# The last 512 rows of a macaron layer on eight cores: x1 + be2 made ahead, ACT's layer norm parts at once, the second MoE by two tiles and then one by one, and a shorter test of the experts

## What is computed

```python
def ffn(x):                       # the MoE; used before and after the attention layer
    out_shared = square(relu(x @ Ws1)) @ Ws2              # 1024 -> 512 -> 1024
    logits = x @ Wr                                       # 8 experts
    top_vals, top_idx = top_k(logits, 2)
    prob = trunc(einsum('tk,tke->te', softmax(top_vals), one_hot(top_idx, 8)))
    out_routed = sum over experts e of prob[:, e] * (square(relu(x @ W1[e])) @ W2[e])
    return out_shared + out_routed

x = x + 0.5 * ffn(layernorm(x))
h = layernorm(x)                                          # tokens of the attention layer
    a = attention(h)                                      # 16 heads of 64, distance bias, Wo, bo
    h1 = layernorm(h + a, g1, be1)
    h2 = layernorm(relu(h1 @ W1 + b1) @ W2 + b2 + h1, g2, be2)   # 1024 -> 4096 -> 1024
x = x + h2
x = x + 0.5 * ffn(layernorm(x))
```

## Time and profile before

| what | value |
|---|---|
| time, median of 3 runs | 1472.01 us (1470.12 to 1521.51) |
| the profiled execution: its own time | 1472.74 us |
| its span, slowest core (core 7) | 1471.2 us |
| spans of the eight cores | 1447.5 to 1471.2 us |
| PE busy | 1302.5 us (89%), 6452 matmuls |
| DVE busy | 790.7 us (54%) |
| ACT busy | 832.0 us (57%) |
| chain that ended last | PE 70%, DMA 8%, DVE 8%, ACT 6%, issue 6%, SP's queue 2% |

### The profile page before, as it was taken

The page is one execution under the profiler, slowest core; times in us unless marked ns, Lnnn a source line. Parts: engine busy times, 40 slices in busy tenths (PEclk is TensorE's granted clock), DMA queues, the critical chain, the costliest instruction groups (busy, mean ns, idle before and its releaser), DMA issues.

```text
span 1471.2 us, 20223 instructions; the slowest of 8 cores (1447.5 to 1471.2 us)
## 1 busy us (share of the span) xinstructions
PE 1302.5 (89%) x6452; PEld 609.8 (41%) x6452; DVE 790.7 (54%) x1272; ACT 832.0 (57%) x1157; POOL 38.3 (3%) x68
## 2 busy tenths in 40 slices
PE   3779679999989999998899999988999999779985
PEld 2334224444433544443335444334454444444432
DVE  5745214554467644358585443775834449670074
ACT  4555337777755765765557567555675666512211
POOL 1011100000000000000000000000000000000000
PEclk9989999999999999999999999999999999999997
DMA  9957989999923522214544222146432323674433
GB/s 238 196 125 140 133 121 131 133 116 115 129 75 105 170 75 101 81 73 154 168 132 128 76 96 90 55 161 211 126 115 74 106 76 78 212 224 171 145 130 116
DMA packets 115214, 187.64 MB, mean 128 GB/s; under 512 B 55822, under 2 KB 92692, under 8 KB 104088
## 3 DMA queue, kind: packets, MB, share of 16 engines
q1 hardware_dynamic: 86536, 154.74, 34.8%
q0 software_dynamic: 28560, 31.45, 17.8%
HBM read 178.86 MB, written 45.09 MB: 152 GB/s over the span
## 4 chain that ended last, share of the span: by engine, by line
PE 70%; DMA 8%; DVE 8%; ACT 6%; issue 6%; SPq 2%; DVEq 0%; ACTq 0%; POOL 0%; POOLq 0%
PE PS L243 70%; DMA Y<-widea 3%; ACT EB L806 2%; DMA HT<-SG 2%; DMA VV<-x 1%; DVE AT L846 1%; DVE EB L812 1%; DMA Y<-SG 1%; DVE Y L1000 1%; DVE sm L224 1%; DVE SG L912 1%; SPq L68 1%; SPq L66 1%; DVE sm L226 1%; ACT RT L842 1%
## 5 line engine op out<-in xcount | busy, mean ns | idle before, releaser
L806 ACT ACTIVATE EB<-PS 128x1024 bf16<-128x1024 f32 x512 | 520.4, 1022 | 323.1 <-PE PS L243 319.8
L812 DVE TENSOR_TENSOR EB<-EB,DP 128x1024 bf16<-128x1024 bf16 x512 | 352.5, 690 | 423.2 <-ACT EB L806 421.8
L243 PE MATMUL PS<-RG,H 128*128 128x512 bf16 x1280 | 314.3, 387 | 28.0 <-ACT H L1033 8.9
L243 PE MATMUL PS<-EB,VV 128*128 128x512 bf16 x1024 | 309.6, 384 | 22.1 <-DVE AT L846 19.1
L243 PE MATMUL PS<-HT,RG 128*128 128x256 bf16 (+1 forms) x1536 | 289.0, 334 | 29.7 <-DMA HT<-SG 13.1
L243 PE MATMUL PS<-QP,KT 128*128 128x512 bf16 x1024 | 309.5, 384 | 5.4 <-ACT EB L806 3.8
L243 PEld LDWEIGHTS PS<-HT,RG 128*128 128x128 bf16 x1536 | 153.3, 100 | 151.5 <-issue 39.0
L243 PEld LDWEIGHTS PS<-RG,H 128*128 128x128 bf16 x1280 | 125.8, 99 | 187.8 <-issue 46.0
L243 PEld LDWEIGHTS PS<-QP,KT 128*128 128x128 bf16 x1024 | 100.4, 99 | 132.0 <-issue 16.1
L243 PEld LDWEIGHTS PS<-EB,VV 128*128 128x128 bf16 x1024 | 96.9, 99 | 139.6 <-issue 47.1
L1033 ACT ACTIVATE H<-PS,sm 128x512 bf16<-128x512 f32 (+1 forms) x160 | 94.8, 599 | 72.6 <-PE PS L243 72.0
(11 more groups left out here) (124 smaller groups left out, 826.1 us busy)
## 6 DMA issues: line engine op xcount, KB each, us to landing
RG<-wcW SPq DMA_DIRECT2D x64, 1024.0 KB, 4.9
RG<-wcWo SPq DMA_DIRECT2D x8, 1024.0 KB, 11.3
wcW<-W1a POOLq DMA_DIRECT2D x8, 1024.0 KB, 22.7
wcW<-W2a POOLq DMA_DIRECT2D x8, 1024.0 KB, 19.8
Y<-x1sp SPq DMA_DIRECT2D x16, 512.0 KB, 4.1
XT<-x1sp SPq DMA_DIRECT2D x16, 512.0 KB, 4.6
RG<-wcS SPq DMA_DIRECT2D x8, 1024.0 KB, 6.7
out<-Y SPq DMA_DIRECT2D x16, 512.0 KB, 3.6
```

The source lines that it names most:

```text
L243: return s.on("tensor", lambda e: e.matmul(out, lhsT, rhs, start=first, stop=last, skip_group_check=True), wait=wait, inc=inc)
L806: te = s.on("scalar", lambda e: e.activation(eb, po, AF.Exp, bias=-12.0, scale=1.0), wait=[tm, self.e_free[k], self.tok_consts])
L812: self.tok_p[k] = s.on("vector", lambda e: e.tensor_tensor(eb3, eb3, dp, ALU.mult), wait=[te, self.tok_dp])
```

## The change

Only the last block (b = 3), where `lagging` is 0, is changed, but for two steps of the test that phase A's router shares.

- First LN: `SG` of tile tt is made in step tt, not in step tt+1.
- x1 of all four tiles is loaded at once after the first LN, into four pieces of `KT` (K is no longer read by then), and be2 is added to all four (4 additions of 1.22 us each, L946) directly after the first LN. `XT` is not used in this block; a tile's second LN goes from L956 straight to L968.
- `ln3_out` (ACT's part of the third LN, and the transposing DMA) is issued as soon as the tile's statistics are, not after those of the next tile.
- The second MoE takes tiles (0, 1), then 2, then 3.
- `router` takes the maximum of `rp1 + rw` (16 numbers a row) instead of the table of 128; the table is made after the flag. In the last block the two `Y` additions of the last tile stand inside the router, behind the exponential on ACT.

```diff
-    def router(self, s, wait, k):
+    def router(self, s, wait, k, mid=None):
...
         te = s.on("scalar", lambda e: e.activation(self.rd, self.rd, AF.Exp), wait=[t])
+        if mid is not None:
+            mid()
...
-        v(lambda e: e.tensor_tensor(PR3, LT3, bc(self.v2), ALU.is_ge))
-        v(lambda e: e.tensor_tensor(PR3, PR3, bc(self.rw), ALU.mult))
-        v(lambda e: e.tensor_tensor(eq3, eq3, bc(self.rp1), ALU.mult))
-        v(lambda e: e.tensor_add(self.PR, self.PR, self.eq1))
+        v(lambda e: e.tensor_add(self.rden, self.rp1, self.rw))
         fm = self.fm[:, k:k + 1]
-        return v(lambda e: e.tensor_reduce(fm, self.PR, AX.X, ALU.max))
+        t = v(lambda e: e.tensor_reduce(fm, self.rden, AX.X, ALU.max))
+
+        def table():
+            v(lambda e: e.tensor_tensor(PR3, LT3, bc(self.v2), ALU.is_ge))
...
+        return t, table
...
-            if tt:
+            j = tt if not self.lagging else tt - 1
+            if 0 <= j < 4:
...
-        tx = self.x1_again(s, b, 0, self.tok_xt_free)
+        if b < 3:
+            txs[0] = self.x1_again(s, b, 0, XT[0], self.tok_xt_free)
+        else:
+
+            XT = [self.KT[:, 2 * D * k:2 * D * k + 2 * D].bitcast(F32) for k in range(4)]
+            for tt in range(4):
+                t = self.x1_again(s, b, tt, XT[tt], [self.q_used[31]])
+                txs[tt] = s.on("vector", lambda e, x=XT[tt]: e.tensor_add(x, x, gc[:, D:2 * D]),
+                               wait=[t, self.tok_gc])
+                yield 1.22
...
             late = tt, Y[tt], c, mv, t
+            if not self.lagging:
+                self.ln3_out(s, b, HTt, *late)
+                late = None
...
-        for lo in (0, 2):
-            yield from self.need(("xn3", b, lo + 1), 3)
-            tr = [self.tok(("xn3", b, tt)) for tt in range(lo + 2)]
+        for lo, hi in ((0, 2), (2, 4)) if b < 3 else ((0, 2), (2, 3), (3, 4)):
+            yield from self.need(("xn3", b, hi - 1), 3)
+            tr = [self.tok(("xn3", b, tt)) for tt in range(hi)]
+            nn = 128 * (hi - lo)
...
+            if 4 * b + tt == 15:
+
+                tflag, table = self.router(
+                    s, [tlt], 1, lambda: [self.moe_out(s, b, tt, dh, *outs[dh]) for dh in range(2)])
+                bk = self.fill_bank()
+                self.tok_flag2 = self.router_flag(s, tflag, [self.bank_free[bk]], 1, self.bank(bk))
+                self.bank_free[bk] = self.tok_flag2
+                table()
```

More of the change, by code:

```diff
@@ L971, in ln3_out, with x1_again @@
         self.put(("xn3", b, tt), tr)
-    def x1_again(self, s, b, tt, wait):
+    def x1_again(self, s, b, tt, dst, wait):
         i = 4 * b + tt
-        return s.dma("sync", "xt", self.XT[:, :], self.x1_d[128 * i:128 * i + 128, :], wait=wait)
+        return s.dma("sync", "xt" if b < 3 else "xt%d" % tt, dst, self.x1_d[128 * i:128 * i + 128, :], wait=wait)
     def post_fill(self, s, b):
@@ L1089, in post_fill @@
                 yield 1
-            if lo:
+            if hi == 4:
                 self.ring_load(s, tm)
             bk = self.fill_bank()
-            for tt in (lo, lo + 1):
+            for tt in range(lo, hi):
                 for dc in range(NDC):
@@ L1106, in post_fill @@
                 self.ht_free = [tm, tx]
-                if b == 3:
-                    tflag = self.router(s, [tlt], 1)
-            for tt in (lo, lo + 1):
-                i = 4 * b + tt
+            for tt in range(lo, hi):
+                outs = []
                 for dh in range(2):
```

69 lines of the change are left out of this document (39 added, 30 removed).

## The result

The changed kernel takes 1454.56 us, median of 5 runs (1453.86 to 1457.86), the kernel before 1470.12 (1466.79 to 1521.51) on the same chip. The ratio is 0.9905, 95% interval 0.9883 to 0.9926: 14.0 us or 0.95% less, within 2% as forecast, but nearly three times the gain forecast and outside the range of 1462 to 1472.5.

The account below looks back on a forecast made before the run. PE's own work was 70% of the chain, so only waits around the first LN and from the second MoE on could move. +1.0 - 4.7 - 2.2 + 1.0 = -4.9 from 1472.0 gave 1467 us, range 1462 to 1472.5.

Parts of the forecast that it names:

- First place: First LN to FFN up pass: early start lost to a wait of some 5 us for W1's piece 1; +1.0 us.
- wcS1: Start of second MoE: its first weights, queued behind tile 1's transposing DMA, land at 1430.6 and set it; -1.0 us.
- The half clock: Second MoE: 16 first down matmuls take 5.0 us instead of 6.55, -1.6; allowance of 0.8 for the single tiles.
- Single tiles: Second MoE: PE does tile 2 while tile 3 is prepared; 0.056 us per matmul, up pass 1.8 us.
- Rival 1: Second MoE: single tiles do not pay, 128-column matmuls being bound by their weight load; +3.4, 1470.5 us; chance 0.2.
- Test: From the copy of the last logits to the flag: 6.2 us instead of 8.4; -2.2 us.
- The end: After the flag: the table makes DVE last at the barrier, with 0.6 us of cover; +1.0 us.
- Rival 2: W1's piece 1 and wcS1 land early, clock stays up, down pass 3.6 us; 1463 us; chance 0.17.
- Rival 3: First LN: W1 and x1 loads delay tile 3's transposing DMA, second half 7 us late; 1473 us; chance 0.1.
- Rival 4: Row work is hidden anyway: only the test and the 128-column passes gain; 1471 us; chance 0.05.

Follow-up runs that it names:

- e1: Changed kernel with the first LN's SG made one tile late again, as before; 1457.03 us.
- e6: Changed kernel with the second MoE's first weights wcS1 loaded ahead of tile 1's transposing DMA; 1461.90 us.
- e8: Changed kernel with ACT's part of the third LN issued one tile late again, as before; 1455.58 us.
- e7: Changed kernel with x1 loaded tile by tile again and be2 added in the second LN, as before; 1465.21 us.
- e9: e6 plus 15 matmuls into an unused bank ahead of the second MoE's first down pass, results unread; 1457.24 us.
- e3: Changed kernel with the four table steps ahead of the flag's copy again; 1458.45 us.
- e4: Changed kernel with the last tile's two Y additions behind the maximum again, so its output DMA is as late as before; 1457.17 us.
- e10: e4 without the output DMA of the last tile, whose 128 output rows are not written; 1463.24 us.

## Why the prediction was wrong

The sum was -4.9 and the last block gained 12.5 us. Taken at the same cuts, in medians of the cores, the missing 7.6 are (the rows are rounded):

| step | forecast | measured | missed |
|---|---|---|---|
| up to the start of the second MoE | +1.0 - 1.0 = 0 | -1.4 | 1.4 |
| from there to its first down pass | -0.8 | -1.8 | 1.0 |
| from there to the last up pass's end | -2.9 | -5.5 | 2.6 |
| from there to the flag | -2.2 | -2.5 | 0.3 |
| flag to end | +1.0 | -1.4 | 2.4 |

- **First place: right in mechanism.** The stop moved from the transposing DMA to piece 1 of W1 and the early start was lost; e1 shows it by undoing it. The size was +0.3 in the median instead of +1.0, and +2.9 on core 7, where PE waited 8.04 us for piece 1, against "some 5". The landing of one load scatters by 2.3 us between cores, and one row of it had been read.
- **wcS1: right in mechanism**, the chain of core 5 has it and e6 takes it away. The MoE started 0.7 us sooner than the term said, beside the 0.7 of the first place: it landed 4.8 to 5.4 us after its issue, where the prediction had taken 6.2.
- **The half clock: the main miss, and the step that failed.** The prediction gave the first down pass 5.0 us, halfway between the rows of 6.55 and 3.61, because "the gap ahead of them is now half as long", and the single tiles an allowance of 0.8. The gap did shrink, from 2.2 to 2.96 us on the cores of before to 1.1 to 1.7 in after. But the pass took the whole 3.61 on every core (3.40 where the trace has 15 of the 16 matmuls), and both single tiles ran at full clock: 1.4 + 0.8 of the 2.6. The up pass ahead of them, which the prediction left at its old length, took 5.3 us instead of 6.2 (medians), which is 0.9 of the 1.0 in the second row. So 3.1 of the missing 7.6 us are the clock's. It isn't a price to be interpolated.
- **What the clock went by.** The length of the stop ahead of a pass alone doesn't set it. Over all runs, 16 down matmuls took 3.61 after every stop up to 2.1 us, and 4.9 to 6.6 after every one of 3.5 or more. In between both are found: after 2.58 us 4.93 and 6.55 on cores 6 and 7 of before, 3.61 on cores of e8, and e7 has both after the same 2.0 us ahead of a pass of 8. What differs between before and e8 is the stop ahead of the up pass, 5.5 to 5.7 us against 2.9. In e7 that one was 6.1 to 7.2, only the second was short (0.9 to 1.8), and the pass took 3.61 too. So either stop made short was enough, on all cores but one (core 0 of e8: 4.58 for 15 of them, after 2.96); in after both are shorter. What decides between the two outcomes of one length stays open. That it is PE's standing still that costs, e9 shows by filling the stop.
- **Single tiles: right, and the row of 0.056 us held.** 32 matmuls took 1.95 with the last one's full length, 1.78 from the first of them to the first logits' matmul, where 1.8 was forecast. Rival 1 had no place. By the rule of the Trainium skill, "TensorE: Matmul & The Clock Gate", "Back-to-back issue gap", an estimate from its 81 ns gives 2.6 us for the pass; the trace does not agree, it shows 1.78.
- **Test: right**, -2.5 for -2.2.
- **The end: wrong in sign.** "DVE has 0.6 us of cover and costs +1.0" was reasoned from the order of the barrier alone. DVE did become the last there, but e3 shows that it costs nothing that can be seen, since a jump made 1.1 us behind the others is itself 0.7 shorter; what fell away was the last output DMA beside the flag's read and the jumps, 1.0 us by e4 against e10. The prediction had noted that the additions move ahead of the flag, and priced them only on DVE.
- **One core.** On core 7 the gain was 8.9, 4.0 more than the sum; the other 3.6 of the 7.6 are what core 7 differs by from the median. Only 1.0 of them lies in the rows that the prediction read (184.97 against 185.94); 2.7 came up in the execution of after, where core 7 waited longest for piece 1. It was the slowest before because it began its last block latest (1286 us); its last block was the shortest of the eight. Where a core begins that block scatters by 14 to 28 us within each kernel, which no part of the change explains.
- **The rivals.** Rival 2 (weights early, clock stays up) came nearest, and by its clock half rather than by the weights, but its 1463 is still 8 us above the result. Rival 3 did not come: the four x1 loads did not delay the second half to its 7 us on any core; 2.9 on core 7 is the largest. Rival 4 falls with e7, which is 5.7 us slower.

The parts of the change, each by undoing it: x1 ahead 5.7 us, single tiles 3.0 up to the last up pass, table behind the flag 1.0, additions inside the router about 0.9, third LN at once 0, early first LN -0.3 to -0.7, which is within the scatter. Each is one profiled execution. They need not add up, since the waits replace each other.

**Still open:** why W1's piece 1 lands 5.3 us after its issue on one core and 7.6 on another, what beside its length makes a stop of 2 to 3 us cost the clock or not, and why DVE's jump is shorter when it is made behind the others. No part was put into the kernel before alone.

## What to carry to other kernels

At the tail of a kernel, where PE waits between short passes, price each stop twice: for its own length and for the clock of the pass behind it, and take both ends as cases rather than their middle, for in these runs the same 2.58 us cost nothing or 2.9. Read the stages of all cores from a common start before pricing anything, for the slowest core may be the slowest by what came before. A gain on a queue is kept only if the next load on it is on time as well; look what stands behind each DMA that is moved.

## What the hardware showed that had not been expected

- Reading one flag from SBUF into a register took 0.29 to 0.33 us on ACT, PE, POOL and DVE in after, 0.60 to 0.80 in before, where the last output was issued 0.06 us ahead of the read, and 0.82 to 1.24 on DVE in e4, 1.1 us behind the issue of an output. Without the DMA (e10) it was 0.32.
- The taken jump on PE took 3.35 to 3.87 us in after, 3.94 to 4.74 in before and 4.45 to 4.61 in e4, with an output in flight; it is most of the 5.05 us from the flag to the end, and no order of the row work touches it. On DVE the same jump took 3.2 us alone (after) and 3.9 together with the others (e3).
- The same stop of 2.58 us ahead of 16 down matmuls left them at 3.61 us on cores of e8 and at 4.93 and 6.55 on two of before.
- Two 1 MB loads issued as a pair behind three transposing DMAs landed after 7.6 and 10.2 us on core 7, after 5.3 to 7.0 and 7.6 to 9.5 on the others, where the page's median for a load is 4.9.
- Filler matmuls (15 of 3.4 us) ahead of a 16-matmul pass brought it from 6.33 to 3.61 us with the start unmoved.
